# The last batch's slot table by sixteen zero-one matmuls, and new orders in five places of an attention and expert kernel

## What is computed

```
xn   = layernorm(x)                                   # x: 8 batches of 512 tokens x 512
out  = x + attention(xn) + ffn(xn)

attention: prev = xn shifted by a token;  xk, xv, xr, xg = xn + (prev - xn) * tm_k, tm_v, tm_r, tm_g
   r, k, v = xr @ Wr.T, xk @ Wk.T, xv @ Wv.T;   g = sigmoid(xg @ Wg.T)
   wkv = scan over the tokens of sums of exp(k) and exp(k) * v, with a decay
   layernorm((sigmoid(r) * wkv * g) @ Wo.T)
ffn: x = rmsnorm(xn);  the 4 best of 32 experts for each token, with softmax weights
   pos = number of earlier choices of the same expert;  valid = pos < 256
   buf[expert, pos] = x[token];   y = (silu(buf @ w_gate) * (buf @ w_up)) @ w_down
   out[token] = sum of weight * y[expert, pos]
            + sigmoid(x @ w_shared_gate) * ((silu(x @ sw_gate) * (x @ sw_up)) @ sw_down)
```

## Time and profile before

| | us |
|---|---|
| median of 3 runs | 1710.62 (1710.24 to 1713.81) |
| the profiled execution | 1709.76 |
| its span | 1707.9 |
| project stage, in the trace | 0 to about 440 |
| expert stage | about 440 to 877 |
| last stage, first batch to its product with Wo | 877 to 985 |
| the rest | 985 to 1708 |

### The profile page before, as it was taken

One profiled execution on the slowest core, in us unless ns is written; L12 is line 12 of the kernel. 1 busy time (PEld: TensorE's weight loads), 2 busy tenths in 40 slices (PEclk: granted clock), 3 DMA queues, 4 the chain that ended last, 5 costly groups with the idle time before them and its releaser, 6 DMA issues.

```text
span 1707.9 us, 26232 instructions
## 1 busy us (share of the span) xinstructions
PE 1648.5 (97%) x8496; PEld 1405.1 (82%) x8496; DVE 1250.4 (73%) x1852; ACT 697.4 (41%) x1216; POOL 847.2 (50%) x703
## 2 busy tenths in 40 slices
PE   6899999999799999999997899999999999999999
PEld 5677887877699999999986788888888888888887
DVE  6788998887555565556577777776887768687776
ACT  5646565654466666666652312121121212112121
POOL 4588777776444444444456544242433524243351
PEclk9999999999899999999999999999999999999999
DMA  4443434324766666666676655455545344433431
GB/s 158 170 172 137 161 145 150 142 106 175 240 228 240 241 244 240 236 226 226 239 263 219 214 191 170 170 174 171 169 146 175 104 150 130 147 113 111 161 101 54
DMA packets 122938, 299.17 MB, mean 175 GB/s; under 512 B 20508, under 2 KB 31772, under 8 KB 118240
## 3 DMA queue, kind: packets, MB, share of 16 engines
q1 hardware_dynamic: 103104, 263.82, 43.9%
q0 software_dynamic: 19456, 33.67, 7.0%
q10 hardware_dynamic: 288, 0.52, 0.1%
HBM read 233.34 MB, written 81.36 MB: 184 GB/s over the span
## 4 chain that ended last, share of the span: by engine, by line
PE 82%; issue 6%; POOL 5%; DVE 4%; DMA 2%; ACT 1%; SPq 0%; POOLq 0%; DVEq 0%; ACTq 0%
PE bank L2095 25%; PE bank L1314 16%; PE bank L2109 13%; PE bank L942 10%; PE bank L1341 8%; PE bank L2126 5%; POOL slot_tokens L373 3%; PE bank L1306 2%; PE bank L884 1%; PE bank L955 1%; DMA s_piece<-in_sw_down 1%; POOL mix L359 1%; PE bank L901 1%; DVE s_wg L1946 1%; DMA s_piece<-in_sw_up 1%
## 5 line engine op out<-in xcount | busy, mean ns | idle before, releaser
L942 PE MATMUL bank<-mix,w 128*128 128x512 f32 x1488 | 354.4, 396 | 8.5 <-DVE ekv L706 4.3
L942 PEld LDWEIGHTS bank<-mix,w 128*128 128x128 f32 x1488 | 279.9, 190 | 70.3 <-issue 7.6
L2095 PE MATMUL bank<-s_zT,s_wu 128*128 128x512 f32 x1056 | 257.7, 393 | 14.4 <-POOL s_wu L1661 9.1
L2109 PE MATMUL bank<-s_wd,s_h 128*128 128x512 f32 x1056 | 253.8, 389 | 1.9 <-DVE s_h L1857 1.9
L2095 PE MATMUL bank<-s_zT,s_wg 128*128 128x512 f32 x1056 | 253.9, 389 | 0.0
L2095 PEld LDWEIGHTS bank<-s_zT,s_wu 128*128 128x128 f32 x1056 | 199.9, 190 | 58.9 <-POOL s_wu L1661 10.8
L2109 PEld LDWEIGHTS bank<-s_wd,s_h 128*128 128x128 f32 x1056 | 198.0, 188 | 43.8 <-DVE s_h L1857 2.3
L2095 PEld LDWEIGHTS bank<-s_zT,s_wg 128*128 128x128 f32 x1056 | 198.0, 188 | 41.6 <-issue 0.5
L1126 POOL TENSOR_TENSOR e_wg<-e_g_in,e_wg 128x1408 fp32r<-128x1408 f32 x31 | 101.1, 3261 | 209.5 <-ACT e_wg L1150 209.5
L1624 POOL DMA_INDIRECT s_picked<-y_rows,s_slot x128 | 140.5, 1098 | 77.9 <-DVE s_total L1907 38.5
L1733 ACT ACTIVATE s_act_g<-bank 128x512 f32<-128x512 f32 x88 | 52.5, 597 | 289.5 <-PE bank L2095 289.4
(11 more groups left out here) (170 smaller groups left out, 2464.6 us busy)
## 6 DMA issues: line engine op xcount, KB each, us to landing
s_wu<-wu_split SPq DMA_DIRECT2D x77, 512.0 KB, 3.4
e_g_in<-in_w_gate SPq DMA_DIRECT2D x32, 704.0 KB, 4.6
e_u_in<-in_w_up SPq DMA_DIRECT2D x32, 704.0 KB, 6.0
e_d_in<-in_w_down SPq DMA_DIRECT2D x32, 512.0 KB, 6.8
y_rows<-e_y SPq DMA_DIRECT2D x32, 512.0 KB, 2.9
s_zT<-zT_parts SPq DMA_DIRECT2D x16, 1024.0 KB, 7.0
zT_parts<-zT_hi SPq DMA_DIRECT2D x8, 1024.0 KB, 6.2
zT_parts<-zT_lo SPq DMA_DIRECT2D x8, 1024.0 KB, 8.5
```

Of the source, the lines that this page charges most:

```text
L942: last = pe.matmul(pj[m][:], w[i][:, w_part, k, m * P:(m + 1) * P], mix[:, i % 2, k, x_part, :], start=(k == 0 and q == 0), stop=(k == KC ...
L2095: last = pe.matmul(into[:], w[:, w_part, k, :], zT[:, x_part, k, :], start=(q == 0 and k == 0), stop=(q == 2 and k == KC - 1))
L2109: last = pe.matmul(yp[j][:], h[:, i, h_part, j * P:(j + 1) * P], wd[f][:, w_part, :], start=(f == 0 and q == 0), stop=(f == NFS - 1 and q ...
```

## The change

Five things, in the order of the program:

1. Round 0: ACT makes the high parts of V's mix ahead of the exponentials, and `make_z(0, 0)` behind `z_hi` and the high parts of G's weight; DVE makes ekv 0 and 1 ahead of R's mixes; `make_z(1, 1)` goes into round 1 behind the last two gates of batch 0.
2. Round 1: POOL makes `norm_scales` ahead of the first six scatters of batch 0, and DVE's `assign(0)` stands behind V's mixes, their low parts and the statistics of batch 2. ACT's `keep_route(0, 0)` goes behind `make_xn`.
3. Rounds 1 to 6: POOL issues one scatter fewer ahead of the last of the next batch's K mixes.
4. Last round: batch 7 isn't scattered. `assign` keeps `oh` and writes its product to `oh_pos`; `fill_parts` on DVE makes zero-one matrices: `place` (for each choice, which of 128 rows of the table is its position) and `column` (for each choice, the expert's column and half, times the token's number in two parts). `fill` on PE multiplies them: 16 bfloat16 matmuls of 128x128 by 128 in one bank, inside the second pair of R. `fill_table` on DVE adds the two parts to the table that SP read, now without batch 7; then `first_index`, and the gathers, ahead of G's mixes. R's low parts are made by POOL in place of the scatters, V's ahead of `choose`. On PE `score`, `turn_score` and `count` come a few steps later, the first turn of rows two steps earlier, and ACT makes two gates of R ahead of G's high parts and two behind. SP reads the table ahead of the first expert's loads.
5. Last stage, first batch: down pieces are asked for two ahead (`AT` 5, 2, 2). SP's loads and ACT's high parts come in the order up, down, gate (before: gate, up, down), and the first down piece is loaded ahead of the scan's inputs. POOL has one down piece between its first gathers, and three `add_base` go from step 0 to steps 2, 4 and 6.

On POOL, at the end of the project stage (`mix` is the low part of the next batch's K, later of R; `slot_tokens` the table), the rows were

The core of the diff:

```diff
@@ gpsimd, one_round and last_round of the project stage
             if second:
-                scatter(b - 1, 1 - half, ahead + 2 * KC, last)
-            scatter(b, half, 0, MORE - KC)
-            mix_lo_among(b + 1, K_, b, half, MORE - KC, MORE)
+                norm_scales(b + 1, 1 - half)
+                scatter(b - 1, 1 - half, 0, MORE)
+                mix_lo_among(b, R_, b - 1, 1 - half, MORE, last)
...
         def last_round():
-            scatter(LAST, FIRST_HALF, 0, NT * TOPK)
+            mix_lo(LAST, R_)
@@ scalar, first_round
+            for k in range(KC):
+                mix_hi(0, V_, k)
             for m in range(KC):
                 exp_k(0, m)
-                mix_hi(0, V_, m)
-            make_z(0, 0)
             for k in range(KC):
                 z_hi(0, k)
                 weight_hi(G_, (k,))
+            make_z(0, 0)
@@ vector
+        def fill_table():
+
+            dve.wait_ge(table_loaded, 16)
+            fill.link(dve.tensor_copy(table_f[:], keep["table"][:]))
+            dve.wait_ge(filled, 1)
+            fill.link(dve.tensor_tensor(table_f[:], table_f[:], xt[1][:, 0:NCT * E], ALU.add))
+            dve.tensor_tensor(keep["table"][:], table_f[:], xt[1][:, NCT * E:2 * NCT * E],
+                              ALU.add).then_inc(table_full, 1)
...
+            if second:
+                norm_stats(b + 1)
+            for k in range(KC):
+                mix_lo(b, V_, k)
             if second:
                 assign(0, 0, 0)
@@ tensor
+        def fill():
+
+            pe.wait_ge(fill_made, 3)
+            for a in range(NT * TOPK):
+                last = pe.matmul(xt[1][:, 0:2 * NCT * E], place[:, a, :], column[:, a].rearrange("p q s -> p (q s)"),
+                                 start=(a == 0), stop=(a == NT * TOPK - 1))
+            last.then_inc(filled, 1)
...
-            project(LAST, K_, 0, {2: lambda: score(LAST), 3: lambda: turn_score(LAST)})
-            project(LAST, K_, 1, {3: lambda: count(LAST)})
-            project(LAST, V_, 0)
+            project(LAST, K_, 0, {3: lambda: score(LAST)})
+            project(LAST, K_, 1, {1: lambda: turn_score(LAST)})
+            project(LAST, V_, 0, {2: lambda: count(LAST)})
             project(LAST, V_, 1)
             project(LAST, R_, 0)
-            project(LAST, R_, 1)
+            project(LAST, R_, 1, {1: fill})
             project(LAST, G_, 0)
-            project(LAST, G_, 1, {3: first_turn})
+            project(LAST, G_, 1, {1: first_turn})
@@ output_stage
-    AT = (AHEAD + 1, 2, 3)
+    AT = (AHEAD + 1, 2, 2)
...
-            if 1 <= f < NFS - AT[G]:
-                load_piece(G, f + AT[G])
-            if 1 <= f < NFS - AT[U]:
-                load_piece(U, f + AT[U])
-            if f < NFS - AT[D]:
-                load_piece(D, f + AT[D])
+            for which in (U, D, G):
+                if 1 <= f < NFS - AT[which]:
+                    load_piece(which, f + AT[which])
```

More of the change, by code:

```diff
@@ L138, in project_stage @@
     wr_at = at("wr_staged", [P, KC, C], 209)
+    place = at("place", [P, NT * TOPK, P], 192, BF16)
+    column = at("column", [P, NT * TOPK, 2, NCT * E], 200, BF16)
+    oh_pos = at("oh_pos", [P, NT * TOPK, E], 184)
+    small = Small(nc, 188)
+    far = small("far", [P, NT * TOPK])
+    near_far = small("near_far", [P, NT * TOPK, NCT])
+    row = small("row", [P, NT * TOPK])
+    of_row = small("of_row", [P, 1])
+    of_tile = small("of_tile", [P, NT])
+    part = small("part", [P, 2, NT * TOPK, NCT])
+    counting = small("counting", [P, P])
+    table_f = small("table_f", [P, NCT * E])
+    small.before(192)
     small = Small(nc, 374)
@@ L553, in first_round @@
                 mix_hi(1, K_, k)
-            make_z(1, 1)
             gate_g(0, 0)
@@ L562, in one_round @@
             gate_g(b - 1, 3)
-            if not second:
+            if second:
+                make_z(1, 1)
+            else:
                 for k in range(KC):
@@ L743, in choose, with assign @@
             dve.tensor_scalar(token_id, token_id, float(T), None, ALU.add)
-        def assign(b, half, uses):
+        def assign(b, half, uses, product=oh):
             route.round(b, CHOOSE)
@@ L774, in assign, with fill_parts @@
             route.end()
+        def fill_parts():
+            fill.round(0)
+            n, a = NT * TOPK, [P, NT * TOPK, P]
+            fill.step(dve.tensor_scalar(far[:], pos[:], float(P), None, ALU.is_ge))
+            fill.step(dve.tensor_scalar(of_row[:], token_id[:, 0:1], float(-LAST * T), None, ALU.add))
+            fill.step(dve.tensor_scalar(of_tile[:], token_id, token_id[:, 0:1], float(LAST * T), ALU.subtract, ALU.add))
+            fill.step(dve.tensor_tensor_scan(counting[:], ones[:], ones[:], -1.0, ALU.mult, ALU.add))
+            fill.join()
+            fill.step(dve.tensor_tensor(near_far[:, :, 1], far[:], valid[:], ALU.mult))
+            fill.step(dve.scalar_tensor_tensor(row[:], far[:], float(-P), pos[:], ALU.mult, ALU.add))
+            fill.join()
+            fill.step(dve.tensor_tensor(near_far[:, :, 0], valid[:], near_far[:, :, 1], ALU.subtract))
+            dve.tensor_tensor(place[:], counting[:].unsqueeze(1).to_broadcast(a), row[:].unsqueeze(2).to_broadcast(a),
+                              ALU.is_equal).then_inc(fill_made, 1)
+            fill.join()
+            fill.step(dve.tensor_scalar(part[:, 0], near_far[:], of_row[:, 0:1], None, ALU.mult))
+            fill.step(dve.tensor_tensor(part[:, 1].rearrange("p (j k) c -> p j (k c)", j=NT),
+                                        near_far[:].rearrange("p (j k) c -> p j (k c)", j=NT),
+                                        of_tile[:].unsqueeze(2).to_broadcast([P, NT, TOPK * NCT]), ALU.mult))
+            fill.join()
+            for q in range(2):
+                dve.tensor_tensor(column[:, :, q].rearrange("p a (e c) -> p a e c", c=NCT),
+                                  oh[:].unsqueeze(3).to_broadcast([P, n, E, NCT]),
+                                  part[:, q].unsqueeze(2).to_broadcast([P, n, E, NCT]), ALU.mult).then_inc(fill_made, 1)
+        def fill_table():
[5 more added lines that the diff above has]
+                              ALU.add).then_inc(table_full, 1)
         def weight_lo(i):
@@ L825, in one_round @@
             gates(b - 1, 2)
+            for k in range(KC):
+                make_mix(b, half, V_, k)
+            if second:
+                norm_stats(b + 1)
+            for k in range(KC):
+                mix_lo(b, V_, k)
             if second:
                 assign(0, 0, 0)
-            for k in range(KC):
-                make_mix(b, half, V_, k)
-            for k in range(KC):
-                mix_lo(b, V_, k)
-            norm_stats(b + 1)
+            else:
+                norm_stats(b + 1)
             for k in range(KC):
@@ L850, in last_round @@
                 make_mix(LAST, FIRST_HALF, V_, k)
-            choose(LAST)
             for k in range(KC):
                 mix_lo(LAST, V_, k)
-            assign(LAST, FIRST_HALF, B // 2 - 1)
+            choose(LAST)
+            for j in (2, 3):
+                dve.wait_ge(z_stored[j], 16 * B)
+            assign(LAST, FIRST_HALF, B // 2 - 1, oh_pos)
             for k in range(KC):
                 make_mix(LAST, FIRST_HALF, R_, k)
-            for k in range(KC):
-                mix_lo(LAST, R_, k)
-            for m in range(KC):
-                make_ekv(LAST, m)
+            make_ekv(LAST, 0)
+            make_ekv(LAST, 1)
+            fill_parts()
+            make_ekv(LAST, 2)
+            make_ekv(LAST, 3)
+            fill_table()
+            first_index()
             for k in range(KC):
                 make_mix(LAST, FIRST_HALF, G_, k)
-            for k in range(KC):
-                mix_lo(LAST, G_, k)
+                if k:
+                    mix_lo(LAST, G_, k - 1)
+            mix_lo(LAST, G_, KC - 1)
             first_weights()
@@ L1687, in first_work @@
             if f == 0:
-                weight_lo(D, 2)
                 gather(0, 0)
-                gather(0, 1)
-                for j in range(1, NT):
-                    add_base(0, j)
             if f < NFS - AT[D]:
                 weight_lo(D, f + AT[D])
+            if f == 0:
+                gather(0, 1)
             if f in (0, 3, 5):
```

80 lines of the change are left out of this document (49 added, 31 removed).

## The result

The changed kernel takes 1699.57 us in the median (1696.32 to 1700.45) against 1710.43 before: a ratio of 0.9932, with a 95% interval from 0.992 to 0.9945. That is 10.9 us less, where 32 were forecast; the range ended at 1690. The profiled execution took 1696.32 us with a span of 1694.5, 13.4 less than the span before.

What follows compares the result with a forecast made beforehand. PE was taken as the bound, with time to win only where it waits or runs slowly. Terms 8.5 + 0.7 + 9.1 + 14.5 = 32.8 us off 1709.76 gave 1677.0, a median of about 1678, range 1665 to 1690.

Steps and rivals of the forecast that it cites:

- Rounds 0 and 1: New orders on ACT, DVE and POOL shorten PE's waits there: 8.5 us won, ends 6 and 12.
- The bound named: Round 1: POOL, nearly without a gap from first scatter to last K mix, limits the gain to 6.7 us.
- the waits for ekv and sr: Early rounds on PE: waits of 4.29 us for ekv and 1.21 us for sr should go.
- Rounds 2 to 6: One scatter moves behind the last K mix, so PE's waits for POOL's mix go: 0.7 us, ends 0 and 1.6.
- Last round: Batch 7's scatters replaced by matmuls, removing the 10.94 us wait for rows: 9.1 us won, ends 5 and 12.5.
- the chain: Last round, fill to gathered rows: index copied at about 415.3, rows ready at 421.2, 4.2 us before they are wanted.
- The wait for ekv behind fill_parts: Last round: PE may wait in R's second pair while DVE runs fill_parts: 1.5 us, ends 0 and 3.
- The fill: Last round on PE: sixteen added bfloat16 matmuls of 128 columns cost 1.5 us, between 0.8 and 2.1.
- keep_score: Last round: the turned score may find ACT's keep_score late behind four mix_hi: 0.5 us, between 0 and 2.5.
- Last stage, first batch: Gate pieces moved to the end of SP's and ACT's order: 14.5 of 19.6 us lost come back, ends 9 and 19.
- the first rival: Last stage is held by DVE and POOL, not loads: about 5 us won there, total 1687; chance 0.20.
- the rivals: Five alternatives: 1687 us (chance 0.20), 1667 (0.17), 1684 (0.09), about 1715 (0.03), nothing measurable (0.02).

## Why the prediction was wrong

Of 32.8 us 13.4 came in the profiled execution. The four terms fell short by 0.6, 5.2 (rounds 2 to 7), 5.5 and 8.1 us; the last and largest is a stretch that the sum put at nothing.

- **Rounds 0 and 1: right, with some luck.** 8.5 us forecast, 7.9 measured. The bound named (POOL's chain up to the last K mix of batch 2) ran from 88.80 to 131.13, and the sum had 88.6 to 132.4. But PE's waits for it stand at R and G of batch 1, not at K of batch 2 as forecast, and the waits for ekv and sr, taken as gone, left 1.67 and 0.71 us.
- **Rounds 2 to 6: wrong in sign, by little.** The step "one scatter moves behind the last K mix" let the wait for POOL's mix go, but I didn't ask who is next. It was xn, behind DVE's statistics: 0.30 us a round. Instead of 0.7 us won, about 1.8 were lost (the later place of batch 7's zT_lo taken off); with the statistics earlier they come back.
- **Last round: the chain was right, a term too small.** The first rows are in time without a wait, as worked out. The wait for ekv behind fill_parts, put at 1.5 us between 0 and 3, was 3.25 with 1.27 us of slow matmuls behind it. fill_parts took 7.8 us where the sum had 6.4, because two small operations stood beside POOL's low parts of R: the prediction said that these would run together and gave it no price. The end of 3 left out that a wait slows what follows, although had shown that. The fill (1.69) and keep_score (0.39) were as taken.
- **Last stage, first batch: the first rival, half way.** Of the 19.6 us lost there 9.0 came back, not 14.5: loads no longer stand ahead of PE, and DVE beside POOL does. The prediction had the row for it, the 7.22 us operation, and made it the ground of the first rival, at a chance of 0.20; in the term itself it counts as the cause of late loads only. The same blocking, shortened to 4 and 5 us, then stood on PE's path itself. The range's lower end was 9.
- **What follows behind project_out: the step that was missing.** The sum took every stretch in which no instruction changes its place as unchanged. The sixteen matmuls also lie in PE's program, ahead of a loop, and moved its jump's target; that cost 8.1 us in the profile. None of the rivals had it. The wait of 0.72 us "issue" in the trace of before was there to be seen, inside a group of matmuls where the program waits for no semaphore.

With the sizes measured, 7.9 + 4.6 + 9.0 - 8.1 = 13.4 us is the profiled execution; the median of the runs is some 2.5 us less favourable. Between profiles of the same code the stall in the last round, the code waits and the clock behind waits differ; which of them makes the 2.5 us is not shown.

## What to carry to other kernels

An instruction added ahead of a hardware loop costs its own time and can cost more at every jump back: look for waits in the middle of a group of matmuls that nothing released, and try some spare instructions ahead of the loop, where the engine waits anyway. When a long wait is taken away, write down for each engine behind it what is late next, and give the slow matmuls that can stand behind a wait a price of their own. A DVE operation with two inputs beside a run of POOL's tensor operations waited for the run here, so put POOL's DMAs between them.

## What the runs showed of the hardware

- Moving PE's code by 32 instructions, with no other difference, cost 9.6 us in the last stretch of a kernel of 1710 us (722.9 to 732.5): waits of 3.91 and 2.31 us and slow matmuls.
- A wait on a semaphore that is already raised is not free on PE: with 24, 32 and 72 instructions of two such waits each the first turn began at 11.61, 12.47 and 16.86 us, 0.11 us for each instruction more.
- DVE's operation with two inputs stayed out while three POOL tensor operations of 1.3 us followed each other (4.72 us in place of 0.67), and in the kernel before for five (7.22). POOL's stayed out in the same way beside a run of DVE's (5.37 in place of 1.3).
- Behind 3.25 us without work PE ran six matmuls at a granted clock of 0.50 (2.93 us in place of 1.66); behind another wait, of 2.80 us, twelve ran at 1.00.
